# Three rows of register numbers merged into one, read by TensorE with one load per two iterations

## The chip, the cores and the metric

One core of a Trainium2 chip. The time is the device time of one execution in microseconds (us). TensorE (PE) multiplies matrices, with its weight loads shown apart (PEld); VectorE (DVE), ScalarE (ACT) and GpSimd (POOL) work elementwise, GpSimd also issues the indirect gathers, SyncE (SP) issues plain transfers.

## The reference, cut to what matters

Four layers of a graph network over 6250 nodes and 100000 edges, each followed by a layer norm: an attention layer applied twice, a normalised sum, a relational attention with 8 heads, and a gated unit. Edges are sorted by their target node. What concerns this case is the weighted sum over the edges of a node, which occurs three times in this form:

```
alpha = ex / z[dst]                                     # attention weights of a GAT layer, twice
out = segment_sum(g[src] * alpha[:, None], dst, N)
...
out = segment_sum(v * attn[..., None], dst, N)          # relational attention, 8 heads
```

## The kernel before

Nodes stand in 49 blocks of 128. Edges stand in 784 tiles of 128, four tiles to a group (`GT = 4`, 196 groups). A tile whose edges reach into two blocks is visited once for each, so there are `VT = 832` visits, taken in 208 iterations of four. For a visit, VectorE makes a one-hot matrix (edge to row of the block) and TensorE multiplies it with the weighted rows of the tile, adding into the PSUM bank of the block (`block % 8`). The four matmuls of an iteration are fp32 and leave two matmul records each, so an iteration is 8 records and a pair of iterations 16.

Which bank a visit adds to, and in the attention sums which of 64 slots of `tmp` holds its rows, depends on the data. The numbers stand in rows of one partition, made once in the set-up by VectorE (lines 815 to 817): `blkv_row` (block of each visit), `bank_row` (block % 8), `wslot_row` (tile % 64). TensorE's sequencer reads them into registers at every even iteration, for two iterations together: the block of the eighth visit (`newest`), eight banks and, in the attention sums, eight slots. Then it waits until ScalarE has freed the banks up to that block (`s_ev`), and before each iteration until VectorE has finished its inputs (`s_wv`).

Three stages do this. `gat_sums` runs twice, for the two attention layers (lines 1580 to 1598 on TensorE). In it GpSimd gathers the rows of those groups that were not gathered earlier (75 groups the first time, 110 the second, four indirect transfers a group), SyncE stores each gathered group to `edge_v` in HBM and brings groups back into `e_values`, and VectorE weights them (lines 1564 to 1566). SyncE's order is fixed: up to three groups are brought for every group stored, then one for one, until group `first + j - 2`; the last three are brought after the last store. The last 12 of the 208 iterations hold no new group: VectorE only makes their one-hot matrices there. A one-hot buffer is free when the matmuls of four iterations before are done. `rel_sums` runs once (line 2710 on TensorE); its rows all stand in `edge_v`, GpSimd copies the weights (line 2677) and VectorE makes the one-hots and the weighted rows (lines 2693, 2697), and these too wait for the matmuls of four iterations before.

All loops are written out; each instruction of the 208 iterations is its own.

Of the kernel before, what the change touches and what calls it, by code (L numbers as in the profile page):

```python
# [23 lines left out]
I32 = mybir.dt.int32  # L24
BF16 = mybir.dt.bfloat16
ALU = mybir.AluOpType
# [7 lines left out]
BLOCKS = -(-N // P)  # L34
# [3 lines left out]
GT = 4  # L38
# [15 lines left out]
WSLOTS = 16  # L54
# [13 lines left out]
VT = TILES + BLOCKS - 1  # L68
# [2 lines left out]
VR = 104  # L71
RC = VT // VR
BANKS = 8
WIDTH = P * TC


# [12 lines left out]
def build(nc, A, out):  # L89
    top = ExitStack()  # L90
    with top:
        def sb(stack, name, shape, dt=F32):
            return stack.enter_context(nc.sbuf_tensor(name, shape, dt))
# [39 lines left out]
        src_v = sb(top, "src_v", [P, VT], I32)  # L133
        tm_v = sb(top, "tm_v", [P, VT])
        blkv_row = sb(top, "blkv_row", [1, VT], I32)
        bank_row = sb(top, "bank_row", [1, VT], I32)
        ends_row = sb(top, "ends_row", [1, P], I32)
        pid = sb(top, "vt_pid", [P, 3])
        deg = sb(top, "deg", [P, NBP])
# [138 lines left out]
        gat = ExitStack()  # L278
# [246 lines left out]


        hi_g = sb(gat, "hi_g", [P, 2, TILES])
        wslot_row = sb(gat, "wslot_row", [1, VT], I32)
        COLS = 3
        gx = sb(gat, "gx", [P, COLS, TILES])  # L530
        zx = sb(gat, "zx", [P, NBP * COLS])
# [5 lines left out]
        with phase() as st:  # L537
# [27 lines left out]
            tile_i = sb(st, "vt_tile_i", [1, VT], I32)  # L565
# [40 lines left out]
            with nc.Block() as block:  # L606
# [145 lines left out]
                def _(dve):  # L752
                    v = nc.vector
# [58 lines left out]
                    v.tensor_tensor(b2, v2, ps_v[0][:, :, 0:HV], ALU.subtract)  # L812
                    v.tensor_copy(tile_i[:, :].rearrange("p (h v) -> p h v", h=2), ps_v[0][0:1, :, 0:HV]).then_inc(s_tabc, 1)
                    dve.wait_ge(s_tabc, 1)
                    v.tensor_scalar(wslot_row[:, :], tile_i[:, :], WSLOTS * GT - 1, None, ALU.bitwise_and)
                    link(v.tensor_copy(blkv_row[:, :], blkb[0:1, :]))
                    v.tensor_scalar(bank_row[:, :], blkv_row[:, :], BANKS - 1, None, ALU.bitwise_and)
                    link(v.tensor_scalar(viota[:, :], blkb[:, :], pid[:, 0:1], None, ALU.is_le))
                    v.tensor_reduce(ends_c[:, :], viota[:, :], AX, ALU.add).then_inc(s_ec, 1)
                    dve.wait_ge(s_tab, 2)  # L820
# [146 lines left out]
        def several(eng, ap, top_value):  # L967

            _, values = nc.values_load_multi_w_load_instructions(
                ap, engines=[eng], min_val=0, max_val=top_value,  # L970
                skip_runtime_bounds_check_because="the row is written by this kernel and clamped to the range there")
            return values

        def group_of(eng, v):
            return eng.value_load(grp_row[0:1, bass.ds(v, 1)], min_val=0, max_val=GROUPS - 1)
# [488 lines left out]
        def gat_sums(l):  # L1464
# [49 lines left out]
            with phase() as st:  # L1514
# [11 lines left out]
                s_ev = sem(st, f"e{l}_banks_free")  # L1526
# [3 lines left out]
                with nc.Block() as block:  # L1530
                    @block.gpsimd
                    def _(pool):
                        keep_gathers(pool, gat_src(l), first, live, k_land, k_st)

                    @block.sync
                    def _(sp):
                        def bring(g):
                            if g >= LOADED:
                                sp.wait_ge(s_wv, g + 1 - LOADED)
                            if g >= first:  # L1540
                                sp.wait_ge(k_st[(g - first) % KEEP], ((g - first) // KEEP + 1) * 16)
                            sp.dma_start(vr[:, g % LOADED, :, :], edge_v[g * P:(g + 1) * P, :].rearrange("p (t d) -> p t d", d=D)).then_inc(s_val[g % LOADED], 16)

                        c = 0
                        for j in range(live):
                            while c < min(3 * j + LOADED, first + j - 2):
                                bring(c)
                                c += 1
                            keep_store(sp, first + j, j // KEEP, j % KEEP, k_land, k_st)
                        for g in range(c, GROUPS):  # L1550
                            bring(g)

                    @block.vector
                    def _(dve):
                        v = nc.vector

                        def step(i, k):
                            n = i * WSLOTS + k
                            if n >= RING:
                                dve.wait_ge(s_o, i * (WSLOTS * GT) + (k + 1 - RING) * GT)  # L1560
                            if n < GROUPS:
                                dve.wait_ge(s_val[k % LOADED], i * (WSLOTS // LOADED * 16) + (k // LOADED + 1) * 16)
                                w = gx[:, :, bass.ds(n * GT, GT)]
                                v.tensor_copy(wv4[:, k, :, D:WCOLS], w.rearrange("p h t -> p t h"))  # L1564
                                v.tensor_tensor(wv4[:, k, :, 0:D], vr[:, k % LOADED, :, :], w[:, 0, :].unsqueeze(2).to_broadcast([P, GT, D]), ALU.mult)  # L1565
                            v.tensor_tensor(oh[:, k % RING, :, :], iota[:, :].unsqueeze(1).to_broadcast([P, GT, P]),  # L1566
                                            drel_v[:, bass.ds(n * GT, GT)].unsqueeze(2).to_broadcast([P, GT, P]), ALU.is_equal).then_inc(s_wv, 1)

                        v.memset(zero[:, :], 0.0).then_inc(s_zero, 1)
                        v.memset(acc[:, BLOCKS * D:NBP * D], 0.0)  # L1570
                        v.memset(zx[:, BLOCKS * COLS:NBP * COLS], 0.0)
                        for k in range(WSLOTS):
                            step(0, k)
                        for i in range(1, GROUPS // WSLOTS):
                            for k in range(WSLOTS):
                                step(i, k)
                        for k in range(WSLOTS):
                            step(GROUPS // WSLOTS, k)
                        dve.wait_ge(s_tk, BLOCKS)
                        finish(dve, None, s_fin, s_e)  # L1580

                    @block.tensor
                    def _(pe):
                        for i in range(0, ITERS // RING):
                            for k in range(RING):
                                n = i * RING + k
                                if k % 2 == 0:
                                    newest = pe.value_load(blkv_row[0:1, bass.ds(n * GT + (2 * GT - 1), 1)], min_val=0, max_val=BLOCKS - 1)
                                    banks = several(mybir.EngineType.PE, bank_row[0:1, bass.ds(n * GT, 2 * GT)], BANKS - 1)
                                    slots = several(mybir.EngineType.PE, wslot_row[0:1, bass.ds(n * GT, 2 * GT)], WSLOTS * GT - 1)  # L1590
                                    pe.wait_ge(s_ev, newest + 1)
                                pe.wait_ge(s_wv, n + 1)
                                for t in range(GT):
                                    bank, slot = banks[k % 2 * GT + t], slots[k % 2 * GT + t]
                                    nc.tensor.matmul(ps_b[:, bass.ds(bank, 1), 0:WCOLS].rearrange("p o d -> p (o d)"), oh[:, k, t, :],  # L1595
                                                     wv[:, bass.ds(slot, 1), :].rearrange("p o d -> p (o d)"),
                                                     start=False, stop=True, skip_group_check=True).then_inc(s_o, 1)

                    @block.scalar
                    def _(act):  # L1600
                        f = nc.scalar.activation
                        act.wait_ge(s_zero, 1)
                        for k in range(BANKS):
                            f(ps_b[:, k, 0:WCOLS], zero[:, :], ACT.Copy).then_inc(s_ev, 1)
                        for b in range(BLOCKS):
                            n = act.value_load(ends_row[0:1, b:b + 1], min_val=1, max_val=VT)
                            act.wait_ge(s_o, n)
                            f(acc[:, b * D:(b + 1) * D], ps_b[:, b % BANKS, 0:D], ACT.Copy)  # L1608
                            f(zx[:, b * COLS:(b + 1) * COLS], ps_b[:, b % BANKS, D:WCOLS], ACT.Copy).then_inc(s_tk, 1)
                            act.wait_ge(s_tk, b + 1)  # L1610
                            f(ps_b[:, b % BANKS, 0:WCOLS], zero[:, :], ACT.Copy).then_inc(s_ev, 1)
                        finish(None, act, s_fin, s_e)
# [1028 lines left out]
        def rel_sums():  # L2641

            W = D + HEADS
            with phase() as st:
# [13 lines left out]
                with nc.Block() as block:  # L2658
# [52 lines left out]
                    def _(pe):  # L2711
                        for i in range(0, rounds):
                            for k in range(RING):
                                n = i * RING + k
                                if k % 2 == 0:
                                    newest = pe.value_load(blkv_row[0:1, bass.ds(n * GT + (2 * GT - 1), 1)], min_val=0, max_val=BLOCKS - 1)
                                    banks = several(mybir.EngineType.PE, bank_row[0:1, bass.ds(n * GT, 2 * GT)], BANKS - 1)
                                    pe.wait_ge(s_ev, newest + 1)
                                pe.wait_ge(s_wv, n + 1)
                                for t, bank in enumerate(banks[0:GT] if k % 2 == 0 else banks[GT:2 * GT]):  # L2720
                                    nc.tensor.matmul(ps_b[:, bass.ds(bank, 1), 0:W].rearrange("p o d -> p (o d)"), oh[:, k, t, :], wv[:, k, t, :],
# [68 lines left out]
```

## Time and profile before

| | us |
|---|---|
| runs of the kernel before: median (lowest, highest) | 6019.24 (6011.39, 6022.19) |
| the profiled execution | 6018.44 |
| its span | 6016.5 |
| first attention sums, within it | about 682 to 1118 |
| second attention sums | about 1614 to 2226 |
| relational sums | about 4582 to 4854 |

The profile is of one execution. The span is the time between its first and last record; 1.9 us lie outside it. TensorE is busy for 61% of the span, VectorE 60%, GpSimd 69%, ScalarE 25%: no engine bounds the whole, each stage has its own bound.

### The profile page before, as it was taken

To read this page: it belongs to the slowest core of one execution; us is meant where nothing else is said; L and a number is where in the kernel's file an instruction comes from. 1 tells how busy PE (TensorE), PEld (TensorE's weight loads), DVE (VectorE), ACT (ScalarE), POOL (GpSimd) and SP (SyncE) were. 2 spreads that over 40 slices of the span, in tenths; PEclk is the share of its full clock that TensorE was granted. 3 is DMA by queue.
4 is the path that set the end of the run, shared out by engine and by line. 5 is a ranking of instruction groups with operands and counts; after the bars stand their busy time and mean duration, and the time that the engine had idled before them with its cause. 6 is when DMAs were issued, how large, how long until landed. Compare 5 with 4: busy or idle time off the path is not lost. (4 is left out here: it accounts for less than half of the span.)

```text
span 6016.5 us, 106908 instructions
## 1 busy us (share of the span) xinstructions
PE 3699.8 (61%) x29332; PEld 3070.5 (51%) x29332; DVE 3610.2 (60%) x10962; ACT 1531.2 (25%) x3918; POOL 4144.0 (69%) x4416
## 2 busy tenths in 40 slices
PE   4765355566364344445555799999975864444556
PEld 2555355455353333445554577777754753344444
DVE  4699475699573235444554788888869952223235
ACT  0476000377100011000000455555540140000004
POOL 6677777377777746777776577777773447777772
PEclk8655698655596555555555899999987985555557
DMA  5687576488585544566772466666663732221221
GB/s 164 179 242 229 159 247 214 132 242 241 160 247 173 151 122 139 165 175 183 189 197 55 142 207 206 206 207 207 207 148 113 205 85 53 53 53 51 53 53 37
DMA packets 564739, 946.34 MB, mean 157 GB/s; under 512 B 122022, under 2 KB 225983, under 8 KB 563599
## 3 DMA queue, kind: packets, MB, share of 16 engines
q0 software_dynamic: 140576, 316.92, 21.1%
q1 hardware_dynamic: 263907, 405.95, 21.0%
q10 hardware_dynamic: 159712, 216.63, 11.7%
q8 instruction: 290, 4.75, 0.3%
q14 instruction: 254, 2.08, 0.1%
HBM read 705.34 MB, written 235.74 MB: 156 GB/s over the span
## 5 line engine op out<-in xcount | busy, mean ns | idle before, releaser
L256 POOL DMA_INDIRECT s_rows<-rel_tab,src_v x832 | 809.6, 973 | 272.5 <-issue 246.7
L256 POOL DMA_INDIRECT stash<-gat_tab,src_g x784 | 780.6, 996 | 251.8 <-issue 238.0
L256 POOL DMA_INDIRECT gcn_rows<-gcn_tab,src_g x784 | 751.9, 959 | 247.9 <-issue 236.2
L256 POOL DMA_INDIRECT ggn_rows<-ggn_tab,src_g x784 | 747.7, 954 | 248.3 <-issue 248.0
L256 POOL DMA_INDIRECT stash<-in_x,src_g x736 | 738.9, 1004 | 236.9 <-issue 223.1
L1595 PE MATMUL e_psb<-tmp,e_oh 128*128 x3328 | 553.4, 328 | 554.9 <-DVE e_oh L1566 459.3
L1595 PEld LDWEIGHTS e_psb<-tmp,e_oh 128*128 128x128 f32 x3328 | 495.7, 231 | 612.9 <-issue 612.8
L2108 PE MATMUL gcn_pso<-gcn_rows,gcn_oh 128*128 x1952 | 500.9, 438 | 484.1 <-SPq L965 396.4
L1940 PE MATMUL ggn_pso<-ggn_rows,ggn_oh 128*128 x1952 | 470.0, 417 | 492.2 <-SPq L965 486.1
L2108 PEld LDWEIGHTS gcn_pso<-gcn_rows,gcn_oh 128*128 128x128 f32 x1952 | 431.2, 325 | 510.2 <-issue 510.2
L1940 PEld LDWEIGHTS ggn_pso<-ggn_rows,ggn_oh 128*128 128x128 f32 x1952 | 405.8, 308 | 557.0 <-issue 557.0
L1163 PE MATMUL g_psc<-g_parts,g_oh 128*128 128x52 bf16 x9408 | 474.2, 221 | 295.1 <-DVE g_oh L1082 272.5
L1163 PEld LDWEIGHTS g_psc<-g_parts,g_oh 128*128 128x128 bf16 x9408 | 425.4, 120 | 344.5 <-DVE g_oh L1082 320.9
L1867 DVE TENSOR_TENSOR acc<-acc,ggn_pso 128x128 f32 x244 | 70.1, 287 | 710.9 <-PE ggn_pso L1940 710.9
L2052 DVE TENSOR_TENSOR acc<-acc,gcn_pso 128x128 f32 x244 | 70.1, 287 | 530.5 <-PE gcn_pso L2108 530.4
L1564 DVE COPY tmp<-gx 128x12 f32<-128x12 f32 x392 | 85.3, 218 | 477.8 <-DMA e_values<-edge_v 405.7
L1055 ACT ACTIVATE acc<-g_lo_rows,g_neg_pid 128x512 f32<-128x512 bf16 x392 | 283.0, 722 | 208.7 <-DVE g_oh L1082 199.1
L1566 DVE TENSOR_TENSOR e_oh<-iota,drel_v 128x512 f32<-128x512 f32 x416 | 283.7, 683 | 17.6 <-PE e_psb L1595 17.6
L2586 ACT ACTIVATE s_hm<-s_psr,tm_v 128x128 f32<-128x128 f32 x832 | 237.8, 368 | 172.7 <-PE s_psr L2521 172.7
L2044 DVE TENSOR_SCALAR gcn_oh<-iota,dst_tab,w_tab 128x128 f32<-128x128 f32 x976 | 279.7, 366 | 0.0
L1608 ACT ACTIVATE acc<-e_psb 128x128 f32<-128x128 f32 x98 | 27.2, 278 | 979.9 <-PE e_psb L1595 979.9
L1565 DVE TENSOR_TENSOR tmp<-e_values,gx 128x512 f32<-128x512 f32 x392 | 268.5, 685 | 0.0
(502 smaller groups left out, 8071.9 us busy)
## 6 DMA issues: line engine op xcount, KB each, us to landing
edge_v<-stash SPq DMA_DIRECT2D x392, 256.0 KB, 2.2
g_lo_rows<-lo_rows ACTq DMA_DIRECT2D x392, 256.0 KB
e_values<-edge_v SPq DMA_DIRECT2D x392, 256.0 KB, 4.2
oh_dram<-tmp ACTq DMA_DIRECT2D x208, 256.0 KB
s_oh<-oh_dram SPq DMA_DIRECT2D x208, 256.0 KB
edge_v<-acc SPq DMA_DIRECT2D x208, 256.0 KB
r_values<-edge_v SPq DMA_DIRECT2D x208, 256.0 KB, 3.0
tmp<-drel_rows ACTq DMA_DIRECT2D x208, 128.0 KB
```

The costliest lines, as they stand in the source:

```text
L256: pool.indirect_dma_start(rows[:, t, :], None, tab[:, :], bass.IndirectOffsetOnAxis(ap=edges[:, t:t + 1], axis=0)).then_inc(s_land, 16)
L1055: nc.scalar.activation(sq[:, k % 2, :], trow[:, k, GE:2 * GE], ACT.Square, bias=neg_pid[:, :]).then_inc(s_sq, 1)
L1163: m = nc.tensor.matmul(ps_c[k % 2][:, a * GT + t, 0:NBP], oh[:, k, a * GE + t * P:a * GE + (t + 1) * P], part[:, a, n, :], start=(n == 0), ...
L1564: v.tensor_copy(wv4[:, k, :, D:WCOLS], w.rearrange("p h t -> p t h"))
L1565: v.tensor_tensor(wv4[:, k, :, 0:D], vr[:, k % LOADED, :, :], w[:, 0, :].unsqueeze(2).to_broadcast([P, GT, D]), ALU.mult)
L1566: v.tensor_tensor(oh[:, k % RING, :, :], iota[:, :].unsqueeze(1).to_broadcast([P, GT, P]), drel_v[:, bass.ds(n * GT, GT)].unsqueeze(2).to_ ...
L1595: nc.tensor.matmul(ps_b[:, bass.ds(bank, 1), 0:WCOLS].rearrange("p o d -> p (o d)"), oh[:, k, t, :], wv[:, bass.ds(slot, 1), :].rearrange( ...
L1867: v_.tensor_tensor(ab, ab, ps_o[k % 2][:, 0:D], ALU.add).then_inc(s_acc, 1)
L1940: m = nc.tensor.matmul(ps_o[k % 2][:, 0:D], oh[:, k % 2, t, :], rows[:, bass.ds(slot, 1), t, :].rearrange("p o d -> p (o d)"), start=(t == ...
L2044: i = v.tensor_scalar(oh[:, k % 2, t, :], iota[:, :], dst_tab[:, col_], w_tab[:, col_], ALU.is_equal, ALU.mult)
L2108: m = mm(ps_o[k % 2][:, 0:D], oh[:, k % 2, t, :], rows[:, bass.ds(slot, 1), t, :].rearrange("p o d -> p (o d)"), start=(t == 0), stop=(t = ...
L2586: m = f(hm[:, h, t, :], ps_r[h][:, t, D:2 * D], ACT.Copy, scale=tm_v[:, bass.ds(n * GT + t, 1)])
```

## The change

The numbers of a pair of iterations are laid side by side: `num_row` holds for each of the 104 pairs 17 numbers (newest block plus one, eight banks, eight slots), `rel_num_row` the first nine of them. VectorE writes both in the set-up: the same two bit operations now write with a step of 17, one small operation adds one to the newest blocks, and a copy of 936 numbers makes the second row. `wslot_row` and `bank_row` are gone; `num_row` is 3744 bytes longer than `wslot_row` was, `rel_num_row` 416 bytes longer than `bank_row`, so that what is allocated behind them moves by that. On TensorE one call reads all numbers of a pair; the range of the first is still checked at run time, and its addition of one is gone.

```diff
+PAIR = 2 * GT
+NUMS = 1 + 2 * PAIR
...
-        bank_row = sb(top, "bank_row", [1, VT], I32)
+        rel_num_row = sb(top, "rel_num_row", [1, VT // PAIR * (1 + PAIR)], I32)
...
-        wslot_row = sb(gat, "wslot_row", [1, VT], I32)
+        num_row = sb(gat, "num_row", [1, VT // PAIR * NUMS], I32)
...
-                    v.tensor_scalar(wslot_row[:, :], tile_i[:, :], WSLOTS * GT - 1, None, ALU.bitwise_and)
+                    nums = num_row[:, :].rearrange("o (m k) -> o m k", k=NUMS)
+                    v.tensor_scalar(nums[:, :, 1 + PAIR:NUMS], tile_i[:, :].rearrange("o (m k) -> o m k", k=PAIR), WSLOTS * GT - 1, None, ALU.bitwise_and)
                     link(v.tensor_copy(blkv_row[:, :], blkb[0:1, :]))
-                    v.tensor_scalar(bank_row[:, :], blkv_row[:, :], BANKS - 1, None, ALU.bitwise_and)
+                    pairs = blkv_row[:, :].rearrange("o (m k) -> o m k", k=PAIR)
+                    v.tensor_scalar(nums[:, :, 1:1 + PAIR], pairs, BANKS - 1, None, ALU.bitwise_and)
+                    link(v.tensor_scalar(nums[:, :, 0:1], pairs[:, :, PAIR - 1:PAIR], 1, None, ALU.add))
+                    v.tensor_copy(rel_num_row[:, :].rearrange("o (m k) -> o m k", k=1 + PAIR), nums[:, :, 0:1 + PAIR])
                     link(v.tensor_scalar(viota[:, :], blkb[:, :], pid[:, 0:1], None, ALU.is_le))
...
+        def pair_numbers(row, m, count):
+            values = several(mybir.EngineType.PE, row[0:1, m * count:(m + 1) * count], WSLOTS * GT - 1)
+            opened = nc.s_assert_within(values[0], 1, BLOCKS)
+            return opened, [bounded(b, BANKS - 1) for b in values[1:1 + PAIR]], [bounded(k, WSLOTS * GT - 1) for k in values[1 + PAIR:]]
+
+        def bounded(value, top_value):
+            return nc.s_assert_within(value, 0, top_value, skip_runtime_bounds_check_because="the row is written by this kernel and clamped to the range there")
...
                                 if k % 2 == 0:
-                                    newest = pe.value_load(blkv_row[0:1, bass.ds(n * GT + (2 * GT - 1), 1)], min_val=0, max_val=BLOCKS - 1)
-                                    banks = several(mybir.EngineType.PE, bank_row[0:1, bass.ds(n * GT, 2 * GT)], BANKS - 1)
-                                    slots = several(mybir.EngineType.PE, wslot_row[0:1, bass.ds(n * GT, 2 * GT)], WSLOTS * GT - 1)
-                                    pe.wait_ge(s_ev, newest + 1)
+                                    opened, banks, slots = pair_numbers(num_row, n // 2, NUMS)
+                                    pe.wait_ge(s_ev, opened)
...
-                                    newest = pe.value_load(blkv_row[0:1, bass.ds(n * GT + (2 * GT - 1), 1)], min_val=0, max_val=BLOCKS - 1)
-                                    banks = several(mybir.EngineType.PE, bank_row[0:1, bass.ds(n * GT, 2 * GT)], BANKS - 1)
-                                    pe.wait_ge(s_ev, newest + 1)
+                                    opened, banks, _ = pair_numbers(rel_num_row, n // 2, 1 + PAIR)
+                                    pe.wait_ge(s_ev, opened)
```

## Rows read from the trace of the kernel before

**Rows 1.** Windows: start:end, length, each engine's busy us (instructions), TensorE clock, DMA share, GB/s.
```profile
682.00:1084.00 402.00, 229.23 (x1536) 207.46 (x1536) 255.56 (x581) 27.94 (x134) 309.78 (x300) 0.86 0.72 224
1084.00:1118.00 34.00, 21.24 (x128) 19.51 (x128) 13.15 (x25) 4.38 (x21) 0.00 (x0) 0.76 0.14 34
1614.00:2192.00 578.00, 282.39 (x1536) 249.94 (x1536) 258.03 (x579) 27.13 (x131) 442.93 (x440) 0.67 0.61 188
2192.00:2226.00 34.00, 20.51 (x128) 18.78 (x128) 12.79 (x25) 4.38 (x21) 0.00 (x0) 0.79 0.14 34
4585.00:4854.00 269.00, 221.44 (x1664) 201.20 (x1664) 260.18 (x415) 30.71 (x146) 105.67 (x204) 0.99 0.70 202
```

**Rows 2.** Waits between 686 and 1084 us: waiter, releaser: total us, times, longest.
```profile
POOL stash L256 <- issue: 90.8, 298, 0.3
DVE tmp L1564 <- PE e_psb L1595: 43.1, 40, 3.7
```

**Rows 3.** Timeline, end of first attention sums: start, us, what, idle before and releaser.
```profile
1082.96 0.94 POOL L256 DMA_INDIRECT stash<-in_x,src_g  x1 [0.30 <-issue]
...
1091.88 2.11 PE L1595 MATMUL e_psb<-tmp,e_oh 128*128 x8 [4.71 <-DVE e_oh L1566]
...
1094.67 6.72 PE L1595 MATMUL e_psb<-tmp,e_oh 128*128 x32 [0.68 <-DVE e_oh L1566]
...
1101.56 2.06 PE L1595 MATMUL e_psb<-tmp,e_oh 128*128 x16 [0.17 <-issue]
...
1106.16 0.69 DVE L1566 TENSOR_TENSOR e_oh<-iota,drel_v 128x512 f32<-128x512 f32 x1 [1.81 <-PE e_psb L1595]
...
1108.39 2.06 PE L1595 MATMUL e_psb<-tmp,e_oh 128*128 x16 [1.37 <-DVE e_oh L1566]
...
1111.81 2.06 PE L1595 MATMUL e_psb<-tmp,e_oh 128*128 x16 [1.36 <-DVE e_oh L1566]
...
1115.17 2.06 PE L1595 MATMUL e_psb<-tmp,e_oh 128*128 x16 [1.30 <-issue]
1117.27 0.28 ACT L1608 ACTIVATE acc<-e_psb 128x128 f32<-128x128 f32 x1 [3.16 <-PE e_psb L1595]
```

**Rows 4.** Sequencer instructions of line 1588, 1104 to 1109 us: durations in ns, start.
```profile
L1588 PEldq TENSOR_LOAD <-blkv_row x1: 306/306/306, 1106.1 to 1106.1; - x1
L1588 PEldq FUSED_REGOPS  x1: 151/151/151, 1106.5 to 1106.5; - x1
```

**Rows 5.** The same for line 969 in that stretch.
```profile
L969 PEldq TENSOR_LOAD <-wslot_row x2: 585/588/591, 1104.0 to 1107.4; - x2
L969 PEldq TENSOR_LOAD <-bank_row x1: 587/587/587, 1106.8 to 1106.8; - x1
```

**Rows 6.** Line 969, whole run: loads of four numbers (line 2526), of eight.
```profile
L969 PEldq TENSOR_LOAD <-blkv_row x416: 330/337/841, 2312.5 to 4456.1; - x139
L969 PEldq TENSOR_LOAD <-bank_row x312: 585/587/1121, 683.2 to 4850.6; - x156
```

**Rows 7.** Timeline, end of the relational sums.
```profile
4848.63 0.69 DVE L2697 TENSOR_TENSOR r_wv<-r_values,r_wv 128x512 f32<-128x512 f32 x1 [0.20 <-POOL r_wv L2677]
4849.02 2.12 PE L2721 MATMUL r_psb<-r_wv,r_oh 128*128 128x136 f32 x16 [0.43 <-ACT r_psb L2736]
...
4849.88 0.68 DVE L2697 TENSOR_TENSOR r_wv<-r_values,r_wv 128x512 f32<-128x512 f32 x1
...
4851.54 2.12 PE L2721 MATMUL r_psb<-r_wv,r_oh 128*128 128x136 f32 x16 [0.40 <-ACT r_psb L2736]
```

**Rows 8.** Waits between 4582 and 4856 us.
```profile
PE r_psb L2721 <- issue: 33.9, 75, 0.6
...
DVE r_wv L2697 <- POOL r_wv L2677: 4.4, 21, 0.5
```

**Rows 9.** Timeline of VectorE in the set-up.
```profile
124.17 0.69 DVE L817 TENSOR_SCALAR bank_row<-blkv_row 1x832 int32<-1x832 int32 x1
...
130.78 1.02 DVE L821 SCALAR_TENSOR_TENSOR drel_v<-vt_blk,vt_psv 128x832 f32<-128x832 f32 x1 [4.30 <-PE vt_psv L648]
```

## The prediction

> **What bounds the kernel now.** I first looked for the stages in which TensorE reads these numbers and cut the profile there by windows [rows 1]. Three stages do it: the two attention sums, 682 to 1118 and 1614 to 2226 us, and the relational sums, 4582 to 4854 us. The reader should see three different pictures in the same loop.
>
> While the attention sums gather, GpSimd issues 300 gathers in 402 us and 440 in 578 us, one every 1.31 to 1.34 us. The waits say that it never stands still for anybody: its idle time is 298 pauses of 0.3 us without a releaser [rows 2]. Had TensorE been slow enough to hold up SyncE's stores, a buffer of `stash` would be missing and GpSimd would wait for it. It does not, so these 402 and 578 us are set by the gathers. VectorE does wait 43.1 us there for TensorE [rows 2], but that is slack inside the gathers' pace.
>
> After the last gather comes a tail of 34 us, in which GpSimd is idle, TensorE is busy for 21.24 and 20.51 us and VectorE for only 13 [rows 1]. The timeline shows what it is made of [rows 3]. The last gather is issued at 1082.96, its group has been stored, brought back and weighted at about 1091.9, and then TensorE runs pair after pair: starts at 1108.39, 1111.81 and 1115.17, so one pair in 3.42 us, of which 2.06 us are matmuls and 1.36 us a gap. VectorE's row at 1106.16 waited 1.81 us for TensorE; so the gap, although the profile names VectorE as its releaser in most rows, is TensorE's own. ScalarE's copy at 1117.27 ends the stage and follows the last matmul directly.
>
> The rows of the sequencer show what it does in the gap [rows 4, 5]. The first load starts at 1106.1 and takes 0.306 us, register work for the range check starts at 1106.5, the load of eight banks at 1106.8 (0.587), of eight slots at 1107.4 (about 0.59), and at 1108.39 the next pair's matmuls start. That is 2.29 us, of which some 0.9 us lie under the matmuls still queued.
>
> The relational sums are nearly balanced: VectorE is busy 260.18 of 269 us, 2.50 us a pair, and TensorE's pairs start 2.52 us apart (4849.02 and 4851.54) with a gap of 0.40 to 0.43 us [rows 1, 7]. Its idle time of 33.9 us has no releaser, which is again its own loads [rows 8]. The end shows that it trails: VectorE is done at 4850.56, TensorE at 4853.66, 3.10 us later, where one iteration of matmuls (1.06 us) would do [rows 7].
>
> **The change, part by part.** *Attention, TensorE.* A pair loses the load of one number, both loads of eight, and the addition; it gains one load of 17 numbers, of duration X. The checks stay. Kept of the 2.29 us are the stretch from the end of the first load to the banks' load (1106.41 to 1106.8, 0.39 us) and from the end of the slots' load to the matmul (1107.99 to 1108.39, 0.40 us), less about 0.1 us that I assume for the addition and its step. So the new chain is X + 0.69, and a pair gains 1.60 - X.
>
> No row shows 17 numbers. Rows give 0.306 for one, 0.337 for four and 0.587 for eight [rows 4, 6]. Lower bound: 0.010 us for each further number, as between one and four, from the eight on: 0.587 + 9 x 0.010 = 0.68. Upper bound: no cheaper than the three loads together, 0.306 + 2 x 0.587 = 1.48; five pieces of four numbers at 0.25 would be 1.34. The step from four to eight is 0.0625 a number, which gives 0.587 + 9 x 0.0625 = 1.15. I take that, since the longest loads are the nearest rows. A pair then gains 0.45 us.
>
> How many gaps does this shorten? In the tail the pairs start at 1094.67, then every 3.4 us to 1115.17: seven pairs, six full gaps of about 1.36 us ahead of six of them, and one of 0.68 us ahead of the first [rows 3]. Seven times 0.45 is 3.2 us a tail. The second tail has the same 128 records and the same length [rows 1]. Two tails: 6.3 us. With X = 0.68 the gain is 0.92 a pair, 0.68 for the first gap: 2 x (0.68 + 6 x 0.92) = 12.4. With X = 1.48 it is 2 x 7 x 0.12 = 1.7. In the gathering parts the gain is nothing, covered by the gathers. VectorE cannot take over the tail: it needs 13 of 34 us.
>
> One published rule bears on X. The rows of eight say 0.587 us, the row of one 0.306 [rows 4, 6]. The Trainium skill, page "DMA: Bandwidth & Descriptors", section "Latency and other measured facts", gives a load of this kind a floor of about 600 ns; the row of one number lies at half of it, so the trace does not agree with it as a floor. As an estimate from that page, a single load of 17 numbers at 0.6 us would gain 1.0 us a pair, some 13 us in the two tails instead of 6.3.
>
> *Relational, TensorE.* A pair loses the load of one and of eight, and the addition, and gains a load of nine: 0.60 (0.587 + 0.010) to 0.89 (0.306 + 0.587), 0.65 by the slope taken above. The chain gains 0.306 + 0.587 + 0.1 - 0.65, about 0.35 us, so that the period could fall from 2.52 to about 2.2 us, at worst to 2.4. VectorE's 2.50 us bind in either case. What is then gained is what VectorE loses through TensorE's lateness, 4.4 us of waits for GpSimd's copies (those wait for the matmuls of four iterations before) [rows 8], and the trailing end: 3.10 us less 1.06 us of matmuls and 0.2 us of handing over, 1.8 us. Together 6.2 us; I take 5.5, because the copies may be late now and then for other causes. Bounds: 1.5, if only the end gains, and 6.2.
>
> *Set-up, VectorE.* The bit operations cover as many numbers as before. New are one small operation and a copy of 936 numbers, together some 1 us by the 0.69 us of the bank row [rows 9]. Behind them VectorE waits 4.30 us for TensorE's table [rows 9]; this hides it. Without that cover it would cost 1 us.
>
> *Addresses.* What lies behind the two rows moves. The trace has no price for that; I put nothing and count up to 3 us either way into the range.
>
> *Sum.* 6.3 + 5.5 = 11.8 us. The profiled execution took 6018.4 us (span 6016.5 and 1.9 outside), so 6006.6 after; it lies 0.8 us below the median of 6019.24, so 6007.4 by the median. I say 6007.
>
> **The rivals.**
>
> *A, the sum above,* X between 0.95 and 1.34 us: two tails 9.1 to 3.6 us, relational 5.5, so 14.6 to 9.1 us less, 6004 to 6010.
>
> *B, a load costs by its round trip and hardly by its numbers,* X from 0.6 to 0.75. For it speaks that one and four numbers differ by only 0.03 us, against it that eight cost 0.25 more than four. Tails 12.4, relational 5.5: 18 us less, 6001. The Trainium skill's floor, named above, read as a flat price would point this way.
>
> *C, the tails gain little or the relational stage keeps its pace.* X of 1.48 or more leaves 1.7 us; if VectorE's waits in the relational sums come from the length of GpSimd's copies, only the end gains, 1.5 us. Between 3 and 8 us less: 6011 to 6016. For it speaks that VectorE is already at 97% of its stage.
>
> *D, slower.* The new loads start at steps of 68 and 36 bytes, where the old ones start at steps of 32. If a load of nine is done as two of eight (2 x 0.587 = 1.17), the relational pair grows by 0.18 us, TensorE becomes its bound, and 104 pairs cost 18 us; the 17 numbers as three such (1.76) cost 0.16 us in 14 gaps, 2 us. That would be 6039. It decides from a nine-number load of 1.0 us on. Against it speaks only that a second pass for every load would be a large price for four bytes more; no row has such starts, so the trace cannot exclude it.
>
> **How the numbers follow.** A 0.50, B 0.22, C 0.22, D 0.06. The likeliest is A, 6007. The range runs from B's 6001 less 2 us of the scatter to the upper end of C with 2 us for the same: 5999 to 6018. It leaves out D and a little on both sides. 0.2% is 12 us and about what the measurement can tell from no change. A's sum lies at that border: a bit under half of A, nearly all of B fall on the faster side, 0.46; the rest of A, C and a very little of B are no change, 0.48; D slower, 0.06.
>
> **What would show it right or wrong.** One load of 17 numbers in each of 208 pairs, and its duration, 1.15 us. The pairs in both tails 3.0 us apart instead of 3.42; tails of 31 us. The gathering parts at 402 and 578 us as before. In the relational sums TensorE's gaps released by VectorE, VectorE's waits for GpSimd's copies near nothing, and the end within 1.3 us of VectorE's. The prediction is wrong if X is outside 0.95 to 1.34, if the gathering parts change length, or if the relational stage does not shorten.

## The result, and the profile after

The changed kernel takes 6333.45 us (median of 5 runs, 6326.8 to 6336.39) beside 6016.94 us for the kernel before: ratio 1.0524, 95% interval 1.0513 to 1.0536. It is 316 us slower. Forecast were 6007 us and a range up to 6018.

The profiled execution has a span of 6324.9 us, 308.4 more than before. The loads stand first, because they were the step priced without a row. These are sequencer rows of line 975 over the whole run (the helper that all such loads go through), with minimum, median and maximum in ns:

```profile
L975 PEldq TENSOR_LOAD <-num_row x208: 1354/4098/7021, 683.5 to 2440.7; - x104
L975 PEldq TENSOR_LOAD <-rel_num_row x104: 842/2167/2194, 4807.1 to 5156.3; - x104
```

The single load of 17 numbers takes 4.1 us where its three predecessors took 0.306 + 2 x 0.587 = 1.48 [rows 4, 5]; that of nine takes 2.17 where 0.89 had been removed. But the minima, 1.354 and 0.842, lie near what was hoped for. The next two rows are the same view cut to one load each, in the end of the first attention sums, where no gather is under way:

```profile
L975 PEldq TENSOR_LOAD <-num_row x1: 4032/4032/4032, 1228.2 to 1228.2; - x1
...
L975 PEldq TENSOR_LOAD <-num_row x1: 1357/1357/1357, 1234.0 to 1234.0; - x1
```

The fast load at 1234.0 belongs to pair 100 of 0 to 103. Its numbers start 100 x 68 = 6800 bytes behind the row's start, a multiple of 16; the loads of pairs 98 and 99 and 101 to 103 do not start at one. The same holds for every pair of the three stages: the 78 loads whose pair number is a multiple of four take at most 1.80 us (17 numbers) and 0.87 us (nine), the other 234 at least 4.03 and 2.16 us. TensorE's timeline of the same place shows the price (start, us, idle before and releaser):

```profile
1227.08 3.32 PE L1609 MATMUL e_psb<-tmp,e_oh 128*128 x16 [2.28 <-issue]
1232.85 2.06 PE L1609 MATMUL e_psb<-tmp,e_oh 128*128 x16 [2.45 <-issue]
1235.91 2.06 PE L1609 MATMUL e_psb<-tmp,e_oh 128*128 x16 [0.99 <-DVE e_oh L1582]
1241.77 3.48 PE L1609 MATMUL e_psb<-tmp,e_oh 128*128 x16 [3.80 <-issue]
1247.57 3.34 PE L1609 MATMUL e_psb<-tmp,e_oh 128*128 x16 [2.31 <-issue]
```

A slow pair is 5.8 us long, the one fast pair 3.06 us, against 3.42 before [rows 3]. Three of four pairs are slow. The matmuls of a pair take 2.06 us in some rows and 3.3 to 3.5 in others, and the granted clock of the first gathering part falls from 0.86 to 0.66; but the clock does not set the pace: with matmuls of 3.48 us a pair is 5.80 us long (1241.77 to 1247.57), with matmuls of 2.06 us 5.86 (1235.91 to 1241.77). The load decides. Windows show where that lands: start:end, length, busy us of each engine, granted clock, DMA share, GB/s; they answer to [rows 1].

```profile
683.50:1207.50 524.00, 308.13 (x1520) 290.33 (x1520) 260.75 (x581) 27.32 (x131) 320.51 (x300) 0.66 0.60 172
1207.50:1256.00 48.50, 26.51 (x144) 24.54 (x144) 13.29 (x24) 4.90 (x24) 0.00 (x0) 0.76 0.12 25
1753.00:2400.00 647.00, 334.87 (x1536) 305.94 (x1536) 261.27 (x576) 26.95 (x130) 451.05 (x440) 0.61 0.56 167
2400.00:2449.00 49.00, 27.92 (x128) 25.56 (x128) 13.64 (x26) 4.35 (x21) 0.00 (x0) 0.60 0.11 24
4810.00:5161.00 351.00, 221.79 (x1664) 201.35 (x1664) 268.30 (x415) 30.39 (x144) 134.76 (x204) 0.99 0.55 155
```

The gathering parts grow from 402 to 524 and from 578 to 647 us, the tails from 34 to 48.5 and 49, the relational sums from 269 to 351: 122 + 69 + 14.5 + 15 + 82 = 302.5 of the 308.4 us. The same 300 and 440 gathers now need more time, and the waits of the first attention sums, 686 to 1207 us, say why (waiter, releaser: total us, times, longest):

```profile
DVE tmp L1580 <- PE e_psb L1609: 248.1, 133, 4.9
...
POOL stash L258 <- DMA edge_v<-stash: 121.4, 43, 7.1
```

and of SyncE's queue, before (686 to 1084 us) and after:

```profile
SPq L1542 <- DVE e_oh L1566: 59.9, 92, 1.5
...
SPq L1558 <- DVE e_oh L1582: 372.5, 176, 5.8
```

GpSimd, which had waited for nobody, now waits 121.4 us for the stores of gathered groups, as much as the part has grown: TensorE is late, so VectorE is (43.1 us before, 248.1 now, [rows 2]), SyncE stands in brings that wait for VectorE (59.9 us before, 372.5 now), and the store behind them in SyncE's order comes late. The relational stage shows TensorE as its bound too, in waits of VectorE that did not exist:

```profile
DVE r_oh L2707 <- PE r_psb L2734: 62.3, 75, 1.0
```

### The profile page after: what moved, and what is told of

The parts are those of the page before. It is cut to its first block and busy times, and to the rows that moved or that the text cites. A ratio compares the mean times of both kernels' runs of the same rounds, so it can differ in the third digit from the quotient of the medians.

```text
span 6324.9 us, 106078 instructions
## 1 busy us (share of the span) xinstructions
PE 3857.8 (61%) x29332; PEld 3233.2 (51%) x29332; DVE 3623.2 (57%) x10964; ACT 1531.2 (24%) x3918; POOL 4193.4 (66%) x4416
## 5 line engine op out<-in xcount | busy, mean ns | idle before, releaser
L1609 PE MATMUL e_psb<-tmp,e_oh 128*128 x3328 | 697.4, 393 | 632.6 <-issue 322.5
L1609 PEld LDWEIGHTS e_psb<-tmp,e_oh 128*128 128x128 f32 x3328 | 646.4, 295 | 683.9 <-issue 683.4
L1954 PE MATMUL ggn_pso<-ggn_rows,ggn_oh 128*128 x1952 | 484.4, 427 | 478.9 <-SPq L971 469.2
L2691 POOL COPY r_wv<-score 128x32 f32<-128x32 f32 x208 | 135.5, 652 | 256.0 <-PE r_psb L2734 212.1
L2734 PE MATMUL r_psb<-r_wv,r_oh 128*128 128x136 f32 x1664 | 221.9, 287 | 134.4 <-DVE r_wv L2711 117.3
L2734 PEld LDWEIGHTS r_psb<-r_wv,r_oh 128*128 128x128 f32 x1664 | 201.3, 191 | 155.0 <-issue 155.0
```

Source lines behind the costliest of these rows:

```text
L1954: m = nc.tensor.matmul(ps_o[k % 2][:, 0:D], oh[:, k % 2, t, :], rows[:, bass.ds(slot, 1), t, :].rearrange("p o d -> p (o d)"), start=(t == ...
L2691: nc.gpsimd.tensor_copy(wv[:, k, :, D:W], score[:, :, bass.ds(n * GT, GT)].rearrange("p h t -> p t h")).then_inc(s_we, 1)
```

## The experiments

All but one set below ran beside the kernel before on a chip where that takes 6013 or 6016 us (13 and 14 runs, none more than 11 us from its median). padded and lean ran seven to twelve times a set; every other kernel was executed once in its set, so its time is read only where it differs by more than that scatter. Two theories were at hand. One: the sequencer takes numbers four at a time when the load starts at a multiple of 16 bytes and one at a time otherwise. The rival: a load of more than eight numbers is slow as such.

**padded.** Alignment alone is restored; everything else of the change stays.

```diff
+STEP = NUMS + 3
+REL_STEP = 1 + PAIR + 3
...
-            values = several(mybir.EngineType.PE, row[0:1, m * count:(m + 1) * count], WSLOTS * GT - 1)
+            values = several(mybir.EngineType.PE, row[0:1, m * step:m * step + count], WSLOTS * GT - 1)
```

The rows become 104 x 20 and 104 x 12 numbers long. To make room, the second is allocated just ahead of `gat` and given back behind `rel`, so memory behind them moves as well.

> As the change, but each pair's 17 numbers start 20 numbers (80 bytes) apart and its 9 numbers 12 numbers (48 bytes) apart, so that every load starts at a multiple of 16 bytes; the second row stands elsewhere in memory. Theory 1 (a load whose address is a multiple of 16 bytes takes its numbers four at a time, about 0.25 us each four; any other takes them one by one, about 0.235 us each): all 208 loads of 17 take 1.35 us, all 104 loads of 9 take 0.85 us, gathers are as before, 6005 to 6014 us. Rival 2 (loads of more than eight numbers are slow, and the quarter that is fast in the changed kernel is fast for another reason, such as its place in the order of instructions): still three of four loads at 4.0 and 2.17 us, about 6330 us.

It took 6002.32 us beside 6013.23: ratio 0.9978 (0.9968 to 0.9988). All loads are fast, at the time that the fast quarter had shown:

```profile
L978 PEldq TENSOR_LOAD <-num_row x208: 1350/1368/2252, 682.4 to 2207.1; - x104
L978 PEldq TENSOR_LOAD <-rel_num_row x104: 836/845/868, 4571.9 to 4832.8; - x104
```

The number of values is the same as in the change, so the rival falls: 17 numbers cost 1.37 us, and the loss of 316 us turns into a gain of 11 by moving starts. The time lies 3 us under the expected 6005 to 6014; where that comes from is taken up at the end of the next section.

**shift4.** The converse: nothing merged, only the start moved.

```diff
-        bank_row = sb(top, "bank_row", [1, VT], I32)
+        bank_all = sb(top, "bank_row", [1, VT + 4], I32)
+        bank_row = bank_all[:, 1:VT + 1]
...
-        wslot_row = sb(gat, "wslot_row", [1, VT], I32)
+        wslot_all = sb(gat, "wslot_row", [1, VT + 4], I32)
+        wslot_row = wslot_all[:, 1:VT + 1]
```

> The kernel before with its three loads, but the rows of banks and of slots begin one number (4 bytes) later. Nothing is merged. Theory 1: each load of eight takes 0.306 + 7 x 0.235 = 1.95 us instead of 0.587; 2.7 us more per pair in the attention sums, 1.36 in the relational sums (TensorE's pair 3.9 instead of 2.52 us, 140 us over 104 pairs); all in all 6350 to 6550 us. Rival 2 (it is the number of values): 6017 us, loads at 0.587. Rival 3 (a load is slow where it crosses a 64-byte line): every second load of eight now crosses one, so half of the loads slow.

The execution took 6536.68 us, within the 6350 to 6550 expected. Both kinds of load of eight went from 0.587 to 1.94 us, all of them (minimum 1.93), and the single number stayed:

```profile
L971 PEldq TENSOR_LOAD <-bank_row x312: 1935/1938/2517, 682.9 to 5366.4; - x156
L971 PEldq TENSOR_LOAD <-wslot_row x208: 1929/1937/2724, 684.9 to 2594.7; - x104
L1590 PEldq TENSOR_LOAD <-blkv_row x208: 302/307/709, 682.1 to 2592.0; - x104
```

Four bytes in the address of two rows cost 523 us, with the code otherwise that of the kernel before. The rival of 64-byte lines, half of the loads slow, falls too.

**probe.** The disputed cost by itself: a helper line for each count and start, four times each, ahead of the relational sums.

```diff
+                        def probe(c, values):
+                            nc.s_assert_within(values[c - 1], 0, BLOCKS - 1)
+
+                        for r in range(4):
+                            probe(1, nc.values_load_multi_w_load_instructions(blkv_row[0:1, bass.ds(r * 32 + 0, 1)], engines=[mybir.EngineType.PE], ...
...
```

> The kernel before with 160 further loads by TensorE ahead of the relational sums: 1, 2, 4, 5, 8, 9, 12, 16, 17, 20 numbers, each starting 0, 4, 8 and 12 bytes behind a multiple of 128 bytes, four times each. Theory 1: at 0 bytes 0.30, 0.32, 0.34, 0.59, 0.59, 0.84, 0.84, 1.09, 1.35, 1.35 us; at 4, 8 and 12 bytes 0.306 + 0.235 for each number after the first: 0.54, 1.0, 1.25, 1.95, 2.17, 2.9, 3.8, 4.05, 4.8 us, equal for the three. Rival 2: the same time at all four starts. Rival 3: slow only where start and count cross 64 bytes: 16 numbers at 4 bytes, 17 and 20 everywhere.

The execution took 6359.52 us, 346 more than the kernel before; the 160 loads and their checks, from 4586.6 to some 4928 us, make up about 341 of it. Rows of single lines: 1 number at starts 0 and 4 bytes; 2 numbers at 0 and 4; 4 numbers at 0 and 4; 5 at 0; 8 at 0 and at 4, 8 and 12 bytes; 17 at 0 and 4.

```profile
L2716 PEldq TENSOR_LOAD <-blkv_row x4: 306/312/312, 4586.6 to 4842.0; - x4
L2717 PEldq TENSOR_LOAD <-blkv_row x4: 296/300/304, 4587.1 to 4842.6; - x4
...
L2720 PEldq TENSOR_LOAD <-blkv_row x4: 550/551/553, 4588.7 to 4844.2; - x4
L2721 PEldq TENSOR_LOAD <-blkv_row x4: 530/530/530, 4589.5 to 4845.0; - x4
...
L2724 PEldq TENSOR_LOAD <-blkv_row x4: 343/343/343, 4591.8 to 4847.3; - x4
L2725 PEldq TENSOR_LOAD <-blkv_row x4: 997/998/1007, 4592.4 to 4847.9; - x4
...
L2728 PEldq TENSOR_LOAD <-blkv_row x4: 593/598/610, 4596.1 to 4851.6; - x4
...
L2732 PEldq TENSOR_LOAD <-blkv_row x4: 593/593/593, 4601.4 to 4856.8; - x4
L2733 PEldq TENSOR_LOAD <-blkv_row x4: 1930/1932/1935, 4602.2 to 4857.8; - x4
L2734 PEldq TENSOR_LOAD <-blkv_row x4: 1930/1930/1930, 4604.3 to 4859.9; - x4
L2735 PEldq TENSOR_LOAD <-blkv_row x4: 1930/1930/1930, 4606.5 to 4862.1; - x4
...
L2748 PEldq TENSOR_LOAD <-blkv_row x4: 1361/1361/1361, 4640.8 to 4896.4; - x4
L2749 PEldq TENSOR_LOAD <-blkv_row x4: 4030/4032/4035, 4642.4 to 4898.0; - x4
```

Medians of all ten counts, in us, at a start of 0 bytes and at 4 (8 and 12 bytes agree with 4 within 0.005):

| numbers | 1 | 2 | 4 | 5 | 8 | 9 | 12 | 16 | 17 | 20 |
|---|---|---|---|---|---|---|---|---|---|---|
| start at a multiple of 16 bytes | 0.31 | 0.55 | 0.34 | 0.60 | 0.59 | 0.85 | 0.85 | 1.10 | 1.36 | 1.36 |
| any other start | 0.30 | 0.53 | 1.00 | 1.23 | 1.93 | 2.17 | 2.87 | 3.80 | 4.03 | 4.73 |

From such a start, every further four numbers cost some 0.25 us behind the first 0.34, and one number left over costs as much as four (5, 9, 17); from any other start, every number behind the first costs 0.23. The expectation missed one thing: two numbers take 0.55 us even at a good start, more than four. That fits numbers left over being fetched one at a time, also at a good start; but no count with two or three left over behind a full four was measured (6, 7, 10 and so on), so it is not shown.

**rel_only** and **attention_only** split the loss. In the first only the relational sums take nine numbers with one load (as in the change; `bank_row` stays for the attention sums, elsewhere in memory), in the second only the attention sums take 17.

```diff
 # rel_only, against the kernel before, in rel_sums
-                                    newest = pe.value_load(blkv_row[0:1, bass.ds(n * GT + (2 * GT - 1), 1)], min_val=0, max_val=BLOCKS - 1)
-                                    banks = several(mybir.EngineType.PE, bank_row[0:1, bass.ds(n * GT, 2 * GT)], BANKS - 1)
-                                    pe.wait_ge(s_ev, newest + 1)
+                                    values = several(mybir.EngineType.PE, rel_num_row[0:1, n // 2 * NUMS:(n // 2 + 1) * NUMS], WSLOTS * GT - 1)
+                                    opened = nc.s_assert_within(values[0], 1, BLOCKS)
...
+                                    pe.wait_ge(s_ev, opened)
 # attention_only, against the changed kernel, in rel_sums
-                                    opened, banks, _ = pair_numbers(rel_num_row, n // 2, 1 + PAIR)
-                                    pe.wait_ge(s_ev, opened)
+                                    newest = pe.value_load(blkv_row[0:1, bass.ds(n * GT + (2 * GT - 1), 1)], min_val=0, max_val=BLOCKS - 1)
+                                    banks = several(mybir.EngineType.PE, bank_row[0:1, bass.ds(n * GT, 2 * GT)], BANKS - 1)
+                                    pe.wait_ge(s_ev, newest + 1)
```

> Only the relational sums take their numbers with one load of nine, 36 bytes apart; the attention sums are as before. Theory 1: three of four loads at 2.17 us; the relational stage 355 us instead of 272, so about 6100 us, and the rest of the loss, some 225 us, stays with the attention sums. Rival 2 gives the same here.

> Only the attention sums take the 17 numbers 68 bytes apart; the relational sums load as before. If the two losses add up, the relational stage is back at 272 us and the whole at about 6240 us (6333 less the 83 to 89 us of the relational part).

> The kernel of attention_only again beside these: about 6240 us if the two losses of the change add up.

rel_only took 6102.29 us, 89 more than 6013.23. attention_only had its first execution on another chip, on which the kernel before takes 7970.25 us; there it took 8153.15 us, 183 more. The second execution, on a chip with 6015.89 us for the kernel before, took 6243.82, 228 more. 89 + 228 = 317: the two losses add up to that of the change.

**one_more_load** asks how much of TensorE's chain the gathers hide.

```diff
                                     slots = several(mybir.EngineType.PE, wslot_row[0:1, bass.ds(n * GT, 2 * GT)], WSLOTS * GT - 1)
+                                    more = several(mybir.EngineType.PE, wslot_row[0:1, bass.ds(n * GT, 1)], WSLOTS * GT + 7)
+                                    nc.s_assert_within(more[0], 0, WSLOTS * GT - 1)
```

> The kernel before, with one further load of a single number and its range check for each pair of the attention sums: about 0.6 us more in TensorE's chain, a pair of 4.0 instead of 3.42 us. If the gathers hide TensorE up to 3.5 us a pair and a stored group of seven buffers gives some slack beyond, the gathering parts grow by 0 to 40 us together and the tails by 14 x 0.6 = 8 us: 6022 to 6065. If the gathers hid it fully, 6025; if TensorE set the pace everywhere, 208 x 0.6 = 125 us, 6140.

> The kernel of one_more_load again beside these: 6022 to 6065 us if the gathers hide TensorE only up to about 3.5 us a pair; 6025 if they hide it fully; 6140 if TensorE sets the pace everywhere.

On the chip with 7970.25 us for the kernel before it took 7986.87 us, on the other 6053.82, 38 more than 6015.89 and within the 6022 to 6065 expected. Windows of the second execution, the two gathering parts and the first tail:

```profile
682.00:1103.00 421.00, 253.32 (x1536) 230.66 (x1536) 258.40 (x579) 27.93 (x134) 318.12 (x300) 0.82 0.72 213
1103.00:1142.00 39.00, 22.87 (x128) 20.68 (x128) 13.71 (x26) 4.38 (x21) 0.42 (x1) 0.71 0.15 34
1638.00:2220.00 582.00, 299.53 (x1536) 266.94 (x1536) 259.90 (x578) 27.03 (x130) 447.88 (x440) 0.66 0.62 186
```

The first gathering part is 19 us longer and the second 4, where 96 pairs with 0.6 us more each would be 58. How much the gathers cover changes inside a part. Here is the second one cut where its first 976 matmul records are done, before (two lines) and with the further load:

```profile
1614.00:1841.00 227.00, 140.02 (x976) 127.42 (x976) 164.28 (x375) 11.51 (x56) 175.19 (x171) 0.92 0.78 242
1841.00:2192.00 351.00, 142.37 (x560) 122.51 (x560) 93.75 (x205) 15.62 (x75) 267.74 (x270) 0.51 0.51 152
...
1638.00:1900.00 262.00, 162.89 (x976) 148.59 (x976) 167.04 (x375) 11.42 (x55) 203.16 (x193) 0.81 0.74 220
1900.00:2220.00 320.00, 136.64 (x561) 118.34 (x560) 92.86 (x204) 15.62 (x75) 244.72 (x248) 0.53 0.52 158
```

The first 61 pairs take 35 us more, 0.57 us each: there, with three groups brought for each one stored, TensorE had next to no slack (a pair starts every 3.6 us, and 3.42 is what it takes in the tail). The last 35 pairs, with one group brought for each one stored, take 31 us less: they are 10 us apart before, and TensorE makes up the delay in that slack. So the cover that I took for whole is nearly nothing in the first stretch and wide in the second.

**lean** spends the new knowledge: exactly 16 and 8 numbers, no padding.

```diff
-NUMS = 1 + 2 * PAIR
+NUMS = 2 * PAIR
...
-            opened = nc.s_assert_within(values[0], 1, BLOCKS)
-            return opened, [bounded(b, BANKS - 1) for b in values[1:1 + PAIR]], [bounded(k, WSLOTS * GT - 1) for k in values[1 + PAIR:]]
+            opened = nc.s_assert_within(values[PAIR - 1], 1, BLOCKS)
+            last = nc.tensor.snap((opened - 1) & (BANKS - 1))
+            return opened, [bounded(b, BANKS - 1) for b in [*values[0:PAIR - 1], last]], [bounded(k, WSLOTS * GT - 1) for k in values[PAIR:]]
```

VectorE writes the newest block plus one over the eighth bank, with one more wait for its own result.

> One load per pair as in the change, but the newest block plus one stands in the place of the eighth bank, which TensorE's sequencer then works out from it: 16 numbers 64 bytes apart, and eight numbers 32 bytes apart in the relational sums, all starting at multiples of 16 bytes without padding. Theory 1 (four numbers per 0.25 us at such a start): 1.10 and 0.59 us a load, some 0.1 us for the extra register step; pairs in the attention tails 2.95 to 3.05 us apart, relational stage 264 to 267 us; 5995 to 6005 us. A rival that every merged load costs more than its parts would give 6017 or more.

> The kernel of lean again, on another chip: in its first run this kernel and the kernel before both took some 7960 us, so transfers set a different pace there. At the pace of 6017 us for the kernel before: 5995 to 6005 us by the four-numbers theory, 6017 or more by the rival that merging costs.

> The padded kernel again, beside lean on the same chip. If it is the loads' time that counts, lean (16 and 8 numbers, 1.10 and 0.59 us) is 2 to 8 us faster than padded (17 and 9 numbers, 1.35 and 0.85 us).

On the chip with 7970.25 us lean took 7960.24, ratio 0.9982 (0.9965 to 1.0), which cannot be told from no change. On the other it took 6000.08 and padded 5999.71 beside 6015.89: ratios 0.997 (0.996 to 0.9981) and 0.997 (0.9959 to 0.9981). Both beat the kernel before by 16 us; they do not differ, although 2 to 8 us were expected between them and lean's loads are shorter:

```profile
L975 PEldq TENSOR_LOAD <-num_row x208: 1101/1110/2052, 682.0 to 2204.2; - x104
L975 PEldq TENSOR_LOAD <-rel_num_row x104: 587/591/596, 4570.2 to 4832.1; - x104
```

In the tail its pairs are 3.0 to 3.1 us apart (here 1094.40, 1097.39, 1100.41), where padded has 3.1 to 3.2:

```profile
1094.40 2.06 PE L1610 MATMUL e_psb<-tmp,e_oh 128*128 x16 [0.44 <-issue]
1097.39 2.06 PE L1610 MATMUL e_psb<-tmp,e_oh 128*128 x16 [0.93 <-DVE e_oh L1583]
1100.41 2.06 PE L1610 MATMUL e_psb<-tmp,e_oh 128*128 x16 [0.96 <-DVE e_oh L1583]
```

Where lean spares 0.25 us of load it adds register steps; what is left is below 0.1 us a pair, over 14 gaps about 1 us, which the runs do not resolve.

## Why the prediction was wrong

**The step that failed** is the price X of a load of 17 numbers. It was put at 1.15 us, by a slope between loads of four and eight, with an upper bound of 1.48, "no cheaper than the three loads together". Nothing stood behind that bound. Three of four loads took 4.0 us and more. For a good start the slope was low and the prediction's other figure, pieces of four numbers, 1.34 us, was right (1.36; even this lies just outside the 0.95 to 1.34 that the prediction had allowed for X). But both rows behind it, of four and of eight numbers, are loads that start at a multiple of 16 bytes: steps of 16 and 32 bytes, in rows that, by their times in the probe and in shift4, begin at such a multiple. Only the single number started elsewhere, and there the start changes nothing (0.31 and 0.30 us in the probe). The change moved the starts of the long loads to steps of 68 and 36 bytes. This stood in rival D, with the right quantity and the wrong price: a second pass, at most 0.6 us, where in fact every number behind the first costs 0.23 us, as if each were fetched by itself. D's deciding point, 1.0 us for nine numbers, is not contradicted (with 0.85 us the relational stage gets shorter, with 2.17 longer) but no run lies closer to it; its 18 us were 89, and its chance of 0.06 rested only on the doubt that four bytes could be so dear.

The Trainium skill, page "DMA: Bandwidth & Descriptors", section "Latency and other measured facts", gives such a load a floor of about 600 ns; the probe's 0.30 us for one and 0.34 us for four numbers lie under it, and the kind of start, which sets everything else, is not in it.

**The cover by the gathers** was a step taken as unconditional. For a shorter pair it holds nearly: padded and lean shorten the gathering parts by 3 to 7 us each, and not by waiting less (see the sum below). For a longer pair it does not: 191 of the 308 us come from the two gathering parts. That GpSimd waits for nobody said that there was slack, not how much; 402 us over 75 groups, at three groups brought for each one stored, would have said 3.6 us a pair against TensorE's 3.42, a cover of 0.15 us, until the brings go one for one.

**The chain of a pair,** X + 0.69 against 2.29, was right: with X = 1.36 it gives a gain of 0.24 and pairs of 3.18 us in the tail; the fast pair of the change has 3.06, padded 3.1 to 3.2. Its count of "six full gaps of about 1.36 us" misreads the rows: there are 0.17 us ahead of 1101.56 and none inside the row of 32 records at 1094.67, where the matmuls themselves take 3.36 us a pair. The pace of 3.42 us holds there all the same, and in the second run of padded the two tails are 1.7 and 2.5 us shorter (from the last gather's issue to the end of ScalarE's last copy into `acc`), where the chain gives 1.7 each.

**The relational sums** were right in mechanism where the loads are fast. The waits of padded there, in its second set of runs, have no row of VectorE waiting for GpSimd's copies (4.4 us before, [rows 8]); from the first load to ScalarE's last copy the stage takes 264.6 us there and 265.5 in lean, against 271.8 before, a gain of 6 to 7 us where 5.5 to 6.2 were forecast. With loads of 2.17 us TensorE became the bound: four pairs, three slow and one fast, take 13.55 us (matmuls start at 4945.89 and, four pairs on, at 4959.44), 3.39 us a pair, and 104 of them are 352 us.

**The set-up** cost nothing, as said: VectorE's new operations take 0.25 and 0.64 us, and its wait for TensorE's table shrinks from 4.30 [rows 9] to 3.44 us.

**The sum** would have been near with aligned loads, in part by luck: 12 us forecast, 11 and 16 measured for padded. With X = 1.36 its terms give 3.4 + 5.5 = 9 us. The second run of padded shows 4.2 us in the tails, 7.1 in the relational sums, and 7 more where the prediction had put nothing: the last gather of the first attention sums is issued at 1078.96 us (1078.23 in its first run, 1076.50 in lean, 1082.96 before), and the gathers of the second end another 3.3 us sooner. No wait has gone there, since GpSimd waited for nobody before. Its gathers themselves are shorter, as this window shows beside the 309.78 us of [rows 1]:

```profile
682.00:1084.00 402.00, 242.20 (x1544) 216.59 (x1544) 255.06 (x582) 27.94 (x134) 304.80 (x300) 0.83 0.72 224
```

Whether fewer collisions with VectorE or the moved addresses shorten them was not tried. Between the stages some 3 us are lost again, whose cause is open too, so that 15.1 us remain of the span.

## What to carry to other kernels

Before instructions are merged, ask what all rows that price them have in common; here it was the start address, and the change was the first to leave it. On this kernel's evidence, numbers that TensorE's sequencer reads should stand in records whose length is a multiple of 16 bytes, in fours: starting the records of 17 numbers 20 numbers apart turned a loss of 5.2% into a gain of 0.2 to 0.3%. And where a cover is claimed, work out its width in us for each stretch with a pace of its own, in the direction in which the change could go wrong.

## What the runs showed of the hardware

A load of registers by TensorE's sequencer has two regimes by its start address, some 0.25 us for every four numbers from a multiple of 16 bytes and 0.23 us for each number from any other start, a factor of 3 at 8 and at 17 numbers; two numbers are dearer than four even at a good start (0.55 against 0.34 us). While gathers run, the slow kind stretches further: 104 of the 156 slow loads of 17 numbers take over 4.1 us and the longest 7.021, where the tails without gathers show 4.03 to 4.04. In the relational sums, which have transfers (DMA share 0.55) but no gathers, the slow loads of nine stay within 2.16 to 2.19 us. And the same kernel before takes 7970 us on one chip and 6016 on others; the gain of lean could not be told from nothing there.
